# Five norm steps over nine parts of x in self attention, and channel mixing begun in the merged loop's drain

## The reference

```python
# layer 0, 16 heads of 16
x = x + attention(LN(x) @ w_qkv + b_qkv, mask) @ w_ao + b_ao
x = x + attention(LN(x) @ w_q, encoder @ w_kv, cross_mask) @ w_co + b_co
x = x + gelu(LN(x) @ w1 + b1) @ w2 + b2
# layer 1, 32 heads of 8: mixing of neighbouring tokens, w, r, k, v, g, then
a = k_t[..., :, None] * v_t[..., None, :]
out = einsum('bhi,bhij->bhj', r_t, u * a + s);  s = a + w_t[..., :, None] * s
x1 = x + groupnorm(out) * g @ Wo.T
# channel mixing
xc = LN(x1);  sx2 = concat([state[:, 0:1] - xc[:, :1], xc[:, :-1] - xc[:, 1:]])
xk2 = xc + sx2 * ffn_maa_k;  xr2 = xc + sx2 * ffn_maa_r
x_out = x1 + sigmoid(xr2 @ Wfr.T) * (square(relu(xk2 @ Wfk.T)) @ Wfv.T)
```

## Time and profile before

| | |
|---|---|
| median of 3 runs (lowest, highest) | 1268.02 us (1267.18, 1268.71) |
| profiled execution, its own time | 1267.79 us |
| its span in the trace | 1265.7 us |
| PE busy | 1149.1 us, 91% |
| DVE busy | 975.2 us, 77% |
| ACT busy | 757.2 us, 60% |
| POOL busy | 600.6 us, 47% |
| granted PE clock, mean | 0.955 |

### The profile page before, as it was taken

How to read it: one execution, slowest core, us unless ns; L and a number is a source line. 1 busy time by engine, 2 the same in 40 slices (tenths; PEclk the granted TensorE clock), 3 DMA queues, 4 the chain that set the end, 5 groups by cost and what they waited for, 6 DMA issues and landing times. The chain is left out here.

```text
span 1265.7 us, 35817 instructions
## 1 busy us (share of the span) xinstructions
PE 1149.1 (91%) x13568; PEld 969.8 (77%) x13568; DVE 975.2 (77%) x1708; ACT 757.2 (60%) x1681; POOL 600.6 (47%) x520
## 2 busy tenths in 40 slices
PE   4899999999999878999999999999999997844998
PEld 3789888888898756787787787788877876633887
DVE  5777777777777611289999998899898998894787
ACT  4777787777777634655566555665555664333442
POOL 4788887877888700333433433434334344220211
PEclk9999999999999959999999999999999997775999
DMA  9300000111111000000000000000000000000011
GB/s 337 107 1 1 0 1 3 37 38 40 41 41 41 19 2 1 1 1 1 1 1 2 1 1 0 0 0 0 0 0 0 1 1 1 1 1 1 33 42 58
DMA packets 25376, 27.09 MB, mean 21 GB/s; under 512 B 2320, under 2 KB 20048, under 8 KB 24912
## 3 DMA queue, kind: packets, MB, share of 16 engines
q1 hardware_dynamic: 25296, 25.99, 6.1%
HBM read 21.79 MB, written 4.19 MB: 21 GB/s over the span
## 5 line engine op out<-in xcount | busy, mean ns | idle before, releaser
L1378 DVE TENSOR_TENSOR_SCAN late_st<-late_wT,late_st 128x512 f32<-128x512 f32 x128 | 183.8, 1436 | 4.4
L819 POOL TENSOR_TENSOR late_xm<-late_mixed,late_xa 128x512 f32<-128x512 f32 x80 | 93.7, 1181 | 158.1 <-DVE late_mixed L1350 148.6
L275 POOL TENSOR_TENSOR att_z<-att_z,att_row_max 128x512 f32<-128x512 f32 x128 | 132.3, 1056 | 2.0 <-DVE att_row_max L596 1.9
L828 POOL TENSOR_TENSOR late_st<-late_st,late_rT 128x512 f32<-128x512 f32 x32 | 40.7, 1273 | 193.1 <-DVE late_st L1378 193.1
L596 DVE TENSOR_REDUCE att_row_max<-att_z 128x8 f32<-128x512 f32 x128 | 87.1, 681 | 55.2 <-POOL att_z L268 55.2
L1372 DVE TENSOR_TENSOR late_st<-psum,late_kT 128x504 f32<-128x504 f32 x128 | 86.8, 678 | 54.3 <-PE psum L1004 49.9
L889 PE MATMUL psum<-w,late_hT 128*128 128x256 f32 x512 | 121.7, 382 | 1.9 <-ACT late_hT L1134 1.9
L880 PE MATMUL psum<-late_glnT,w 128*128 128x256 f32 x512 | 119.2, 388 | 2.2 <-ACT late_glnT L1124 2.2
L497 ACT ACTIVATE att_probs<-att_z 128x512 f32<-128x512 f32 x128 | 80.8, 631 | 66.9 <-POOL att_z L275 66.8
L889 PEld LDWEIGHTS psum<-w,late_hT 128*128 128x128 f32 x512 | 94.9, 190 | 19.9 <-issue 5.5
L880 PEld LDWEIGHTS psum<-late_glnT,w 128*128 128x128 f32 x512 | 97.4, 195 | 16.1 <-ACT late_glnT L1124 2.9
(11 more groups left out here) (167 smaller groups left out, 2779.8 us busy)
## 6 DMA issues: line engine op xcount, KB each, us to landing
att_encT<-in_enc SPq DMA_DIRECT2D x64, 128.0 KB, 2.6
out<-x SPq DMA_DIRECT2D x16, 256.0 KB, 2.0
x<-in_x SPq DMA_DIRECT2D x6, 512.0 KB, 10.9
w<-in_w SPq DMA_DIRECT2D x2, 1024.0 KB, 17.1
cross_mask<-in_cross_mask SPq DMA_DIRECT2D x1, 1024.0 KB, 12.1
w_qkv<-in_w_qkv SPq DMA_DIRECT2D x1, 768.0 KB, 4.4
x<-in_x SPq DMA_DIRECT2D x1, 768.0 KB, 5.8
w_kv<-in_w_kv SPq DMA_DIRECT2D x1, 512.0 KB, 13.0
```

Source lines behind the costliest of these rows:

```text
L275: nc.gpsimd.tensor_tensor(zs, zs, peak.unsqueeze(2).to_broadcast([P, PAIRS, S]), ALU.subtract).then_inc(shifted, 1)
L819: nc.gpsimd.tensor_tensor(xm[:, m % 2, :, :].rearrange("p h (b t) -> p (h b) t", t=S), mixed[:, m % 2, :, :].rearrange("p h (b t) -> p (h ...
L1378: nc.vector.tensor_tensor_scan(states, wT[:, u, half, :, :, :].rearrange("p j b t -> p (j b t)"), states, 0.0, ALU.mult, ALU.add).then_inc ...
```

## The change

Three things are done.

1. x comes in nine parts, `(2, 2, 4, 4, 4, 4, 4, 4, 4)`, and self attention's norm is made in five: tiles 0 to 1, 2 to 3, 4 to 7, 8 to 11 and 12 to 31. Only the first is ahead of the steps. Two tables, `STATS_AT` and `NORM_AT`, say in which step each `load_stats`, `variances` and `invert_deviations` stands. Four more steps are written out on every engine, and the loop of self attention is one round shorter.
2. In VectorE's body `load_stats`, `variances` and `shifts` now stand right behind `apply_mask`, ahead of `find_max`; in ScalarE's, `invert_deviations` stands at the end.
3. `channel_phase` and its norm phase are gone. Their work is in `late_phase`: the norm of runs 0 to 12 is made in steps 14 and 15 of the merged loop, the first channel runs begin in step 15, and the drain of runs 14 and 15 is written out between channel steps 0 to 3. Each of the four products has one PSUM bank. ScalarE now normalises and squares, GpSimd shifts, and the sigmoid is a tanh of half the argument, in the table set of the merged loop, with its 1 and 0.5 folded into the two finishing instructions on VectorE. The norm of runs 13 to 15 follows channel step 3.

```diff
-X_PARTS = (2, 6, 4, 4, 4, 4, 4, 4)
+X_PARTS = (2, 2, 4, 4, 4, 4, 4, 4, 4)
...
-    LN_PARTS = [(0, 2), (2, 8), (8, TILES), (0, 24), (24, TILES)]
-    SELF_NORMS, FIRST_CROSS, ALL_NORMS = 3, 4, 5
+    LN_PARTS = [(0, 2), (2, 4), (4, 8), (8, 12), (12, TILES), (0, 24), (24, TILES)]
+    SELF_NORMS, FIRST_CROSS, ALL_NORMS = 5, 6, 7
+    STATS_AT = {2: -4, 3: 0, 4: 1, 5: 2, 6: 2, 7: 3, 8: 4}
+    NORM_AT = {1: -5, 2: -3, 3: 1, 4: 4, 5: TILES - 7, 6: TILES}
...
                     apply_mask(*on(k, t, 3), u + 3)
+                for i in STATS_AT:
+                    if n_is(n, STATS_AT[i]):
+                        load_stats(i)
+                for i in NORM_AT:
+                    if n_is(n, NORM_AT[i]):
+                        variances(i)
+                    if n_is(n, NORM_AT[i] + 1):
+                        shifts(i)
+                if there(*on(k, t, 3)):
                     find_max(*on(k, t, 3), u + 3, 0)
...
# VectorE, the merged loop's body and what follows it
+                    if s_is(s, RUNS - 2) and n == 4:
+                        ch_variances(0)
+                    if s_is(s, RUNS - 1):
+                        if n == 0:
+                            ch_shifts(0)
+                        if n == 6:
+                            ch_mix(0, 0)
...
+            def ch_mix(r, u):
+                dve.wait_ge(ch_sx_ready, r + 1)
...
# TensorE
+            def ch_keys(r, u):
+                pe.wait_ge(ch_mixed_ready, r + 1)
+                if not later(r):
+                    pe.wait_ge(gate_done, RUNS)
+                else:
+                    pe.wait_ge(ch_relu_ready, r)
...
+            def channel(s, u):
+                if there(s + 2):
+                    ch_transpose(s + 2, u)
+                if there(s + 1):
+                    ch_keys(s + 1, 1 - u)
+                ch_values(s, u)
+                if there(s + 1):
+                    ch_receptances(s + 1, 1 - u)
 
             bodies(pe, body)
+            project_out(RUNS - 2)
+            sum_heads(RUNS - 1, 2)
+            sum_heads(RUNS - 1, 3)
+            ch_transpose(2, 0)
+            transpose_o(RUNS - 1)
+            ch_keys(1, 1)
+            ch_values(0, 0)
+            ch_receptances(1, 1)
+            channel(1, 1)
+            transpose_on(RUNS - 1)
+            channel(2, 0)
+            project_out(RUNS - 1)
+            channel(3, 1)
+            channel_runs(pe, channel)
...
# ScalarE
+            def channel(s, u):
+                if there(s + 2):
+                    ch_copy_in(s + 2, u)
+                if there(s + 3):
+                    ch_normalise(s + 3, 1 - u)
+                if there(s + 1):
+                    ch_nonlinear(s + 1, 1 - u)
```

More of the change, by code:

```diff
@@ L704, in group, with late_phase @@
     return q % HALVES, q // HALVES * JQ + part * JG
-def late_phase(core):
+def late_phase(core, out):
     nc = core.nc
@@ new lines, in ch_receptances @@
+            def ch_receptances(r, u):
+                if not later(r):
+                    pe.wait_ge(kv_ready, RUNS * GROUPS_R - 1)
+                else:
+                    pe.wait_ge(ch_rr_ready, r)
+                for c in range(CH):
+                    for kb in range(HALVES):
+                        last = nc.tensor.matmul(ch_recept[:, c * C:(c + 1) * C], ch_xr[:, u, kb, c * P:(c + 1) * P],
+                                                w["WfrT"][:, kb, :], start=(kb == 0), stop=(kb == HALVES - 1))
+                last.then_inc(ch_recept_ready, 1)
@@ new lines, in ch_values @@
+            def ch_values(r, u):
+                pe.wait_ge(ch_kk_ready, r + 1)
+                if not later(r):
+                    pe.wait_ge(kv_ready, RUNS * GROUPS_R)
+                else:
+                    pe.wait_ge(ch_rv_ready, r)
+                for c in range(CH):
+                    for kb in range(HALVES):
+                        a = kb * RT + c * P
+                        last = nc.tensor.matmul(ch_value[:, c * C:(c + 1) * C], ch_kk[:, u, a:a + P],
+                                                w["WfvT"][:, kb, :], start=(kb == 0), stop=(kb == HALVES - 1))
+                last.then_inc(ch_value_ready, 1)
@@ new lines, in ch_normalise @@
+            def ch_normalise(r, u):
+                act.wait_ge(norm_ready, norm_of(r))
+                if later(r - 1):
+                    act.wait_ge(ch_xnT_ready, r - 1)
+                for c in range(CH):
+                    t = r * CH + c
+                    last = nc.scalar.activation(ch_xn[:, u, c, :], core.x[:, ds(t, C)], ACT.Identity,
+                                                scale=core.rstd[:, ds(t, 1)], bias=core.neg_mean[:, ds(t, 1)])
+                last.then_inc(ch_xn_ready, 1)
@@ new lines, in ch_copy_in @@
+            def ch_copy_in(r, u):
+                act.wait_ge(ch_xnT_ready, r + 1)
+                if later(r - 1):
+                    act.wait_ge(ch_mixed_ready, r - 1)
+                for half in range(HALVES):
+                    nc.scalar.activation(ch_xc[:, u, half, :, 1:S + 1],
+                                         ch_tr[:, half * RT:(half + 1) * RT].rearrange("p (b t) -> p b t", t=S),
+                                         ACT.Identity, scale=col(core, "r_ln2_w", half), bias=col(core, "r_ln2_b", half))
+                nc.scalar.activation(ch_xc[:, u, :, :, 0], core.state_rows[:, 0, :, ds(r, RB)],
+                                     ACT.Copy).then_inc(ch_xc_ready, 1)
@@ L1444, in body, with channel @@
+            def channel(s, u):
+                if later(s):
+                    ch_finish(s - 1, 1 - u)
+                if there(s + 2):
+                    ch_mix(s + 2, u)
             def body(s, u):
```

405 lines of the change are left out of this document (204 added, 201 removed).

## The result

| | before | change |
|---|---|---|
| median, run side by side (lowest, highest) | 1267.60 us (1265.39, 1268.71) | 1251.88 us (1250.86, 1252.62) |
| profiled execution, its own time | 1267.79 us | 1252.62 us |
| its span | 1265.7 us | 1250.8 us |
| PE busy | 1149.1 us | 1152.3 us |
| ACT busy | 757.2 us | 780.6 us |

The ratio is 0.9879 (95% interval 0.9864 to 0.9894): 15.7 us less, where 19.3 were forecast. The time is 3.2 us over the forecast of 1248.7 and inside the range (1241 to 1257).

What follows compares the result with a forecast made beforehand. TensorE was taken to bound attention's steady steps and channel mixing, with a mostly idle drain between. 16.8 (channel mixing) + 2.1 (start) + 0.4 (large norm steps) = 19.3 us less, forecast 1248.7 us, range 1241 to 1257.

Steps and rivals of the forecast that it cites:

- Keys 0: First channel mixing product on TensorE, in the drain: forecast to start at 1140.4, with 1.3 us for step 14's norm.
- The work of channel mixing: TensorE from its first keys on: channel work unchanged at 94.3 us, plus 5.7 us for the drain's products and transposes.
- The waits: Channel mixing's waits at two table-set changes, 2.2 and 2.0 us, plus 0.3 for a copy: 4.5 us.
- the late phase: Channel mixing begun in the recurrence's drain: last values end at 1244.9 instead of 1261.7, 16.8 us less.
- the start: Self attention's first steps: 4.5 + 4.1 - 5.0 - 1.5 = 2.1 us gained.
- the two large steps: Attention's later norm steps, moved from behind find_max to behind the mask: 0.2 us gained for each, 0.4.
- before's loss of 4.1: Time lost at the ramp's end, score 0 to score 3, in the kernel before: 4.1 us, claimed gone.
- The 1.5 for idle time without a cause: Attention's start: waits for instructions while weight transfers fill the queues, between 0 and 3.7, taken as 1.5 us lost.
- the norm work that delays: Attention steps 1, 2 and 4: statistics and norm on VectorE delay the next score by 1.7, 1.6, 1.7: 5.0 us.
- The rival that the start gives nothing: Attention's start: transfers or instruction fetch hold early steps, attention 2 us slower instead of 2.5 faster, 1253; chance 0.17.
- 1246.5: Total time if moving the two large norm steps saved the 1.43 us wait, without the VectorE and GpSimd lock rule.
- The clock rival: Channel mixing in the drain: waits keep TensorE's clock low, five products more cost 10 us, 1259; all ten, 1269; chance 0.13.

Runs made afterwards that it cites:

- e7: The change with VectorE's drain queue reordered, ScalarE's two inversions with table loads behind its other work, and the drain's last output a step later: 1243.27 us, ratio 0.9808.
- e9: The change with VectorE's drain queue reordered, table loads behind ScalarE's work, and the early norm moved into VectorE's idle time: 1239.94 us, ratio 0.9781.
- e12: The kernel before, unchanged, measured once more for another profile of its start: 1265.6 us (one).
- e10: The change's self attention with the late phase and channel mixing of the kernel before: 1265.47 us, ratio 0.9986.
- e3: The change with VectorE's drain queue reordered, ch_finish ahead of the drain's sum of squares, last residual with statistics and norm, and last shift: 1247.06 us, ratio 0.9839.
- e6: The change with VectorE's drain queue reordered and the later phases' weights held until the first residual: 1246.53 us, ratio 0.9835.
- e4: The change with the start's statistics and norm steps behind the second find_max instead of behind the mask: 1257.97 us, ratio 0.9927.

## Why the prediction was right, and where not

**Keys 0: right, by two errors.** Forecast 1140.4 in before's time, and in a profile whose attention ended as before's they started at 1140.44. That it fits so well is luck. The norm in step 14, with what it delayed, cost 2.05 us in this pair of profiles (1.5 to 2.75 over the others) where I took 1.3; the four mixes took 2.43 where I took 2.9.

**The work of channel mixing: a little too dear.** 94.3 + 5.7 = 100.0 forecast, 98.2 found (e7; 97.5 in e9, where receptances 0 took 2.30 instead of 2.99). The base of 94.3 was the slower of two: e12 and e10, the same channel mixing, took 93.2, with receptances 0 in 1.89 us instead of 3.09. And a step is 5.62 us in the change, where I kept 5.81.

**The waits: the term that was too small.** 4.5 forecast; 5.1 of idle time, 8.2 with the low clock and all that the waits cost. Two mechanisms, and I had one. ScalarE's round with its table loads is real, and sized rightly: e3 leaves it alone, at 4.4 us (2.2 + 2.0 forecast), at the two named places, and e7 removes it. What the working put at nothing is VectorE's queue, 3.8 us: with one bank for values, `ch_finish` is what TensorE waits for next, and it was queued behind the drain's own work. I had asked which engine has too much to do in a step, not what stands ahead of the one instruction that frees a bank. e3 gave 3.8 us back without a single instruction less. The sum closes: 98.2 + 4.4 + 3.8 = 106.4.

So the late phase gave 14.8 us by the first two profiles, and 13.7 with e12 for before, where 16.8 were forecast. With 1.8 for attention that is 15.5 to 16.6, and 15.7 were measured.

**Attention: near in size, wrong in its parts.** 2.1 + 0.4 forecast for the start and the two large steps; 1.8 measured for both together (e10). By e3's profile against before's, both at full clock, the two large steps give 1.1 (0.4 forecast), though the wait for GpSimd moved with them as forecast (L570 at 207.62 took 1.30 in the change, L565 in the earlier trace rows 1.09). The start gives 0.97 at tile 5, where 2.1 were forecast. Its terms: the score is 4.85 us earlier (4.5 forecast), and before's loss of 4.1 is credited in full. The 1.5 for idle time without a cause is the term that was too small: as the sum credits all of the 4.1, with the 1.86 in it, the 1.5 stands for the whole of that idle time, and it was 2.72 there. That leaves 4.85 + 4.1 - 2.72 - 0.97 = 5.3 for the norm work that delays (5.0 forecast), lost mostly at tiles 1 and 4, where statistics and norm instructions stand together. A second idle time of 2.4 us ahead of score 1, which before does not have, stood in six of seven profiles of this attention. It has no price here: score 1 came 6.2 us behind score 0 with it (e3) and 6.5 without it (the change).

The rival that the start gives nothing put attention 2 us over before's. e10's interval, 0.6 to 2.9 us less, excludes that. It does not exclude that the start alone gives nothing: without the 1.1 of the two large steps it is -0.5 to 1.8.

One figure of the prediction is off by its own numbers: two steps that save 1.43 each, less the 0.4 taken, make 1246.2 and not 1246.5.

The forecast had weighed the Trainium skill (Runtime: NRT & Kernel Launch, section "Instruction fetch mechanics"), by which crossing into new instructions is mostly hidden. If the idle time inside step 0's projection is a wait for instructions, which is not shown, the trace does not agree for this start: 2.4 to 2.7 us stood there in all seven profiles of this attention with the weights in flight, and none in the two where they were held. The one ahead of score 1 stood in one of these two as well (e6, 2.43). The other rule of the Trainium skill (SBUF — State Buffer, section "SBUF: two separate sides"), that a VectorE operation with two SBUF inputs and a GpSimd operation that reads SBUF lock each other out for a whole instruction, held in a new place too. L1684, on six columns, took 1.02 us while GpSimd's shift ran (1173.90, 1.04); the neighbours on VectorE took 0.16 to 0.17.

**The clock rival: in small.** It was given 0.13 with five products at the lower clock. Behind the wait of 1.93 us two products ran slow.

## What to carry to other kernels

Where a product has one bank, list for each engine what is queued ahead of the instruction that frees it; put that instruction first and everything that is not due behind it, table loads too. Look in the trace for a stretch where the engine idles before adding small work to its busy one: six instructions cost about 2 us with what they delayed in one, and nothing measurable in the other. Price a wait by how far apart the starts are, not by its idle time alone: waits of 3.2 us cost 4.4. And where a few us at a start decide, take several profiles: identical attention code ended 4.3 us apart.

## What the runs showed that was not expected

TensorE's clock at a start full of short waits is not a property of the program: the first score took 1.11 us behind an idle time of 2.15 in the change, and 0.70 behind one of 2.36 in e9. And the same small norm steps cost 6 us more behind `find_max` than behind the mask (e4), although VectorE does the same work: behind the mask they fill six waits of 0.79 us for GpSimd.
